# Front of a cross-attention and FFN kernel: value banks, turns of the ring, and new orders on all engines

## The reference

```python
x = x + xattn(layernorm(x), ctx, ctx, Wq, bq, Wk, bk, Wv, bv, Wo, bo)
x = x + ffn(layernorm(x), gate_w, gate_z, gate_s, up_w, up_z, up_s, down_w, down_z, down_s)

# xattn, per sample:  q = Wq @ x + bq (64 x 512), k and v from ctx alike
# heads split the 512 columns into 8 times 64
scores = einsum('hbdk,hbek->hbde', qh, kh) / sqrt(64)
out    = Wo @ (softmax(scores) @ vh) + bo
# ffn:  W = (int_w - zeros) * scales, per group of 128 rows; 512 -> 1792 -> 512
ffn(x) = (silu(x @ gate) * (x @ up)) @ down
```

## Time and profile before

| | us |
|---|---|
| time, median of 3 runs | 416.19 (416.04 to 419.14) |
| the profiled execution | 416.88 |
| its span in the trace | 415.1 |
| TensorE busy | 399.7 (96%) |
| VectorE busy | 333.5 (80%) |
| ScalarE busy | 323.5 (78%) |
| GpSimd busy | 263.6 (64%) |
| first gate/up matmul of the main part | 44.73 |

### The profile page before, as it was taken

How to read it: one execution, slowest core, us unless ns; L and a number is a source line. 1 busy time by engine, 2 the same in 40 slices (tenths; PEclk the granted TensorE clock), 3 DMA queues, 4 the chain that set the end, 5 groups by cost and what they waited for, 6 DMA issues and landing times.

```text
span 415.1 us, 10255 instructions
## 1 busy us (share of the span) xinstructions
PE 399.7 (96%) x3923; PEld 315.1 (76%) x3923; DVE 333.5 (80%) x587; ACT 323.5 (78%) x534; POOL 263.6 (64%) x283
## 2 busy tenths in 40 slices
PE   8988999999899999999999999999999999999994
PEld 5866778787677778777778778787778788888872
DVE  3677558889799978899899778898996768877676
ACT  2545898787678888787689888787799999999970
POOL 5374598677977665576667665665766666566550
PEclk9999999999999999999999999999999999999999
DMA  6399999985980010342222000242111002320003
GB/s 222 115 276 199 285 271 267 277 269 115 251 231 27 2 25 4 98 158 87 86 86 77 2 25 2 89 142 77 60 46 51 0 2 76 128 76 26 2 1 101
DMA packets 40250, 44.97 MB, mean 108 GB/s; under 512 B 3810, under 2 KB 29578, under 8 KB 40202
## 3 DMA queue, kind: packets, MB, share of 16 engines
q1 hardware_dynamic: 32242, 36.87, 27.2%
q0 software_dynamic: 7456, 7.34, 11.2%
q10 hardware_dynamic: 504, 0.11, 0.1%
HBM read 35.34 MB, written 8.97 MB: 107 GB/s over the span
## 4 chain that ended last, share of the span: by engine, by line
PE 75%; DVE 8%; issue 5%; POOL 5%; DMA 4%; SPq 0%; POOLq 0%; ACT 0%; DVEq 0%
PE banks L906 22%; PE banks L908 20%; PE banks L919 10%; PE banks L920 10%; PE banks L793 3%; DVE yT L1194 3%; DMA yT<-in_L_ffn_down_z 2%; DMA wgu<-in_L_ffn_up_w 2%; PE banks L810 2%; PE banks L850 2%; PE banks L938 2%; PE banks L839 1%; PE banks L820 1%; POOL hr L510 1%; PE banks L828 1%
## 5 line engine op out<-in xcount | busy, mean ns | idle before, releaser
L678 ACT ACTIVATE banks<-banks,ratio 128x512 f32<-128x512 f32 x336 | 207.2, 661 | 37.2 <-PE banks L908 27.5
L906 PE MATMUL banks<-xT,wgu 128*128 128x512 f32 x448 | 180.2, 402 | 1.5 <-issue 0.9
L1194 DVE SCALAR_TENSOR_TENSOR yT<-banks,sd,yT 128x512 f32<-128x512 f32 x208 | 153.1, 744 | 35.2 <-PE banks L920 34.8
L908 PE MATMUL banks<-xT,wgu 128*128 128x512 f32 x448 | 174.8, 390 | 0.0
L497 POOL TENSOR_TENSOR t_sb<-t_sb,u_sb 128x512 f32<-128x512 f32 x56 | 73.7, 1316 | 64.9 <-DVE t_sb L1179 64.6
L906 PEld LDWEIGHTS banks<-xT,wgu 128*128 128x128 f32 x448 | 84.0, 188 | 23.8 <-issue 3.0
L908 PEld LDWEIGHTS banks<-xT,wgu 128*128 128x128 f32 x448 | 84.2, 188 | 15.7
L919 PE MATMUL banks<-hr,wd 128*128 128x512 f32 x224 | 87.9, 392 | 1.6 <-POOL hr L510 1.6
L920 PE MATMUL banks<-hr,wd 128*128 128x512 f32 x224 | 87.3, 390 | 0.0
L510 POOL TENSOR_TENSOR hr<-t_sb,hr 128x512 fp32r<-128x512 f32 x56 | 73.6, 1315 | 5.1 <-ACT hr L700 0.7
L919 PEld LDWEIGHTS banks<-hr,wd 128*128 128x128 f32 x224 | 42.0, 188 | 12.0 <-DVE yT L1194 2.2
(11 more groups left out here) (114 smaller groups left out, 386.8 us busy)
## 6 DMA issues: line engine op xcount, KB each, us to landing
wgu<-z_out SPq DMA_DIRECT2D x14, 512.0 KB, 6.2
swap_d<-xn SPq DMA_DIRECT2D x18, 256.0 KB, 2.0
x_sb<-swap_d SPq DMA_DIRECT2D x72, 64.0 KB, 2.0
x_sb<-in_x SPq DMA_DIRECT2D x16, 256.0 KB, 5.1
out<-x_sb SPq DMA_DIRECT2D x16, 256.0 KB, 2.2
wgu<-in_L_ffn_gate_w POOLq DMA_DIRECT2D x7, 512.0 KB, 10.9
wgu<-in_L_ffn_up_w POOLq DMA_DIRECT2D x7, 512.0 KB, 11.7
wd_in<-in_L_ffn_down_w SPq DMA_DIRECT2D x7, 512.0 KB, 9.0
```

What stands on the lines that cost most here:

```text
L678: act.activation(banks[:, bank, :], banks[:, bank, :], ACT.Copy, scale=ratio[:, m, g, it:it + 1]).then_inc(done[n % 2], 1)
L906: pe.matmul(banks[:, bank, :], w, xT[:, c % 2, 0, g, :], start=g == 0, stop=False, skip_group_check=True)
L908: pe.matmul(banks[:, bank, :], w, xT[:, c % 2, 1, g, :], start=False, stop=True, skip_group_check=True).then_inc(full[n % 2], 1)
L1194: dve.scalar_tensor_tensor(y, bank, sd[:, it, b:b + 1], y, ALU.mult, ALU.add).then_inc(s_free, 1)
```

## The change

The banks of the values: `values(t)` of the front wrote banks 6 and 7 and now writes banks 4 and 5, for tile 3 banks 2 and 3. The third turn of the ring (tile 2) goes to bank 5 instead of bank 4, and the first turns wait accordingly. On all four computing engines the calls of the front stand in a new order, and TensorE stirs at fewer places. SyncE's order is the same.

```diff
@@ banks and ring
             if kind == "QK":
                 return 0 if t < PRE else 2 if t == PRE else 6
+            if kind == "V":
+                return 6 if t >= PRE else 4 if t < PRE - 1 else 2
             return 2 if t < PRE and kind == "S" else 6
...
             if slot[u] < PRE:
-                return RING_BANK
+                return RING_BANK + (slot[u] == PRE - 2)
...
             if s < PRE:
-                return s
+                return (0, 1, 0)[s]
@@ GpSimd
+            prepare()
             weigh(0)
-            prepare()
             weigh(1)
             add_weights(0)
+            add_weights(1)
+            rstd(0, 4)
             rstd(1, 0)
             weigh(2)
-            add_weights(1)
+            add_weights(3)
             add_weights(2)
+            weigh(3)
             rstd(1, 1)
-            weigh(3)
             rstd(1, 2)
             ratios()
-            rstd(0, 4)
             rstd(1, 3)
-            add_weights(3)
@@ ScalarE
             norm1(0)
             take_qk(0)
-            norm1(1)
             act.wait_ge(s_zraw, 32)
             act.activation(z_neg, z_raw.bitcast(I32), ACT.Copy, scale=-1.0).then_inc(s_zneg, 1)
-            norm1(2)
-            power_of(0)
+            norm1(1)
             act.wait_ge(s_trs, 1)
...
-                if h == 0:
-                    take_qk(PRE)
-
+            take_qk(PRE)
             act.wait_ge(s_prep, 1)
@@ TensorE
-                    mm = pe.matmul(banks[o, 6 + b, 256:512], wT[r, 0, :], ctx_of(t)[r, g * 256:(g + 1) * 256],
+                    mm = pe.matmul(banks[o, pair("V", t) + b, 256:512], wT[r, 0, :], ctx_of(t)[r, g * 256:(g + 1) * 256],
...
-            stir(2)
-            score(0)
-            project_wide(1)
-            stir(2)
             pe.wait_ge(s_sc, 48)
...
-            stir(1)
+            score(0)
+            project_wide(1)
             pe.wait_ge(s_wT, 3)
+            pe.wait_ge(s_scl, 2)
             values(0)
...
@@ VectorE
...
-            rest_x(0)
-            shift(1, 1)
+            shift(0, 4)
             residual(2)
             stats(1, 2)
-            stats(0, 4)
+            shift(1, 1)
+            rest_x(0)
             shift(1, 2)
-            rest_x(1)
-            shift(0, 4)
             residual(3)
             stats(1, 3)
+            rest_x(1)
+            shift(1, 3)
             rest_x(2)
-            shift(1, 3)
             take_qk(4, 0)
```

More of the change, by code:

```diff
@@ L637, in take_v @@
                     act.wait_ge(s_bA, t - 1)
-                act.activation(v_sb[:, t % 2, :, :], banks[:, 6:8, 256:512], ACT.Identity,
+                at = pair("V", t)
+                act.activation(v_sb[:, t % 2, :, :], banks[:, at:at + 2, 256:512], ACT.Identity,
                                bias=bvo[:, 0:1]).then_inc(s_v, 1)
@@ L719, in _ @@
             act.copy(sd[:, :, :].rearrange("p g c -> p (g c)"), banks[:, 4, ng:ng + NI * NC]).then_inc(s_scl, 1)
+            norm1(2)
+            power_of(0)
             take_qk(1)
-            norm1(3)
             act.wait_ge(s_wT, 3)
             take_v(0)
+            norm1(3)
             power_of(1)
+            take_qk(2)
             take_a(0)
-            take_qk(2)
-            take_qk(3)
             take_v(1)
             power_of(2)
+            take_qk(3)
             take_a(1)
             norm2(0)
+            take_v(2)
             power_of(3)
-            take_v(2)
+            take_a(2)
+            take_v(3)
+            norm1(4)
             take_x(0)
-            take_a(2)
+            take_a(3)
             norm2(1)
-            take_v(3)
+            norm2(2)
             take_x(1)
-            take_a(3)
-            norm2(2)
-            norm1(4)
             take_x(2)
@@ L978, in _ @@
             score(1)
-            stir(1)
-            stir(1)
-            wait_qk(pe, 1)
             project_wide(2)
-            pe.wait_ge(s_v, 1)
+            pe.wait_ge(s_sub, 2)
+            stir(1, 2)
             mix(0)
+            score(2)
             apply(0)
-            pe.wait_ge(s_sub, 2)
-            wait_qk(pe, 2)
-            score(2)
+            values(1)
             project_wide(3)
-            stir(1)
             pe.wait_ge(s_x1, 1)
-            values(1)
-            stir(1)
-            stir(1)
-            stir(2)
-            pe.wait_ge(s_v, 2)
             mix(1)
             pe.wait_ge(s_sub, 3)
+            stir(2, 2)
             score(3)
             apply(1)
+            values(2)
+            stir(2, 0)
             pe.wait_ge(s_x1, 2)
-            values(2)
-            pe.wait_ge(s_scl, 2)
-            turn_x(0)
-            pe.wait_ge(s_v, 3)
-            mix(2)
-            stir(1)
-            apply(2)
-            stir(2)
+            mix(2)
+            pe.wait_ge(s_sub, PRE)
+            values(3)
+            stir(2, 0)
+            apply(2)
+            turn_x(0)
+            stir(2, 0)
             pe.wait_ge(s_x1, 3)
-            values(3)
-            stir(3)
+            mix(3)
+            stir(3, 0)
+            apply(3)
             turn_x(1)
-            pe.wait_ge(s_v, 4)
-            mix(3)
-            stir(1)
-            apply(3)
-            stir(2)
-            stir(3)
-            stir(1)
             turn_x(2)
-            stir(1)
-            pe.wait_ge(s_sub, PRE)
             project_wide(PRE)
-            pe.wait_ge(s_free, PRE - 1)
             for h, (n, done) in enumerate(((s_lastn, s_lastX), (s_xn2, s_full))):
+                pe.wait_ge(s_free, (PRE - 2, PRE - 1)[h])
                 pe.wait_ge(n, (1, PRE)[h])
@@ L1031, in _ @@
                 mm.then_inc(done, 1)
-            stir(3, U_BANK[0])
+            stir(2, U_BANK[0])
             for q in range(PLACES):
@@ L1222, in _ @@
             shift(0, 0)
+            stats(0, 1)
             dve.wait_ge(s_brow, 1)
             dve.tensor_copy(bqk[:, :, :].rearrange("p m o -> p (m o)"), banks[:, 7, 0:2 * D]).then_inc(s_bqk, 1)
-            stats(0, 1)
             stats(0, 2)
+            shift(0, 1)
             dve.wait_ge(s_bqk, 1)
             take_qk(0, 0)
-            shift(0, 1)
             stats(0, 3)
             shift(0, 2)
+            take_w(1)
+            dve.tensor_copy(bvo[:, :], banks[:, 7, 4 * D:4 * D + 2]).then_inc(s_wT, 1)
             most(0)
             less_max(0)
+            shift(0, 3)
             take_qk(1, 0)
-            take_w(1)
-            dve.tensor_copy(bvo[:, :], banks[:, 7, 4 * D:4 * D + 2]).then_inc(s_wT, 1)
-            shift(0, 3)
             invert(0)
@@ L1241, in _ @@
             take_qk(2, 0)
+            invert(1)
+            most(2)
             dve.wait_ge(s_wT, 3)
             residual(0)
-            most(2)
-            invert(1)
-            take_qk(3, 0)
             less_max(2)
             stats(1, 0)
+            take_qk(3, 0)
+            stats(0, 4)
             invert(2)
```

## The result

The changed kernel takes 413.82 us (median of 9 runs, 411.9 to 415.59), the kernel before beside it 417.63 (9 runs, 415.77 to 419.14). The ratio is 0.9901, 95% interval 0.9876 to 0.9926: some 4.1 us less by the ratio, 3.8 by the medians. The forecast was 417.4, no change that a measurement can tell; what happened is a gain of 1%, between rival B (415.4) and rival C (410.0 to 412.0). The profiled execution took 413.61 (span 411.8) against 416.88 (span 415.1).

A forecast was written before the change was run, and what follows sets the result against it. Two chains, the front's ladder and a DMA chain, were taken to meet at tile 5's projection burst; 416.88 - 0.8 (DMA chain) + 2.0 (clock fall) = 418.1 profiled, 417.4 median. The 8-in-10 range was 411.0 to 420.2.

The forecast's parts named there:

- rival B: DMA chain holds the burst as in the main forecast, but the clock stays full: 415.4 us, chance 0.25.
- rival C: Down zeros land at 43.3 to 45.3 and most of the front's gain goes through: 410.0 to 412.0 us, chance 0.20.
- Two chains: The front's ladder and a chain of DMAs meet before tile 5's projection burst at 52.43 us.
- the burst of tile 5: TensorE's projection burst in the early main part, at 52.43 before; forecast at 51.6, a gain of 0.8 us.
- the ladder: Front's projection, scores, mix, apply per attention tile; first gate/up matmul forecast at 38.95, 5.8 us earlier than 44.73.
- the DMA chain: Adds 0 and 1, then zeros and down loads; down zeros forecast at 48.7 instead of 49.53, gaining 0.8 us.
- 5.4 us of hole: TensorE's idle time before tile 5's burst, waiting for the down zeros: forecast 5.4 us instead of 0.45.
- a hole under 2 us: Sign before tile 5's burst that the forecast is wrong: the DMA count was wrong and rival C holds.
- Two blocks of zeros and two of adds at 235 per us: DMA queues from 25.6 us: 8.7 us of packets plus 1.5 to landing, so `s_wgu[1]` at 35.8 instead of 38.00.
- The reason behind the sum: The two DMA queues take turns, so an add put in earlier slows the loads beside it.
- a fall after 5.4 us of idling: TensorE's clock falls to 1.2 GHz in the hole before tile 5's burst, costing 0 to 4 us, taken as 2.0.
- the signs named beforehand: Trace milestones in ladder, DMA and TensorE given as tests, such as a 4 to 6 us hole before tile 5's burst.

The follow-up runs named there:

- late_adds: Changed kernel with GpSimd issuing add 1 behind weigh(2) and add 3 behind the last rstd, as before the change; 412.89 us, ratio 0.9898.
- before_again: The kernel before, unchanged, run and profiled once more; 418.2 us.
- adds_alone: Kernel before with only the DMA side of the change: zero points negated earlier, adds 1 and 3 issued earlier; 417.29 us, ratio 0.997.
- before_subs_late: Kernel before with VectorE's first two zero-point subtractions moved behind steps 5 and 7 instead of 2 and 4; 418.25 us, ratio 1.0.
- old_negate: Changed kernel with ScalarE's negation of the zero points put behind norm1(1) again; 415.53 us, one run.
- subs_late: Changed kernel with VectorE's first two zero-point subtractions moved behind steps 5 and 7 instead of 2 and 4; 413.14 us, ratio 0.9868.
- held_zeros: Changed kernel with SyncE holding the zero loads until apply(0) is done; 422.7 us.
- shifted: Changed kernel with two stirring matmuls ahead of the first projection replaced by 34 matmuls of 16 columns; 429.3 us.

## Why the prediction was wrong, point by point

**What bounds it: right.** Two chains meet at the burst of tile 5; what it gains goes through to the end.

**The two chains: the ladder was worked out 1.75 us too early, the DMA chain 2.3 us too late.** The forecast had 5.4 us of hole; 5.4 - 1.75 - 2.3 = 1.35, and 1.34 was there. By the forecast's own sign, a hole under 2 us, the DMA count was wrong; that rival C would then hold did not come true.

**The ladder.** This execution ran 1.14 ahead of that of before from the start (transposes at 10.23 where I began at 11.37). Less that, the steps were forecast at 17.8 for mix(0), 24.2 for apply(1), 27.2 for mix(2), and 37.8 for the first gate/up matmul; they came at 17.83, 27.23, 28.92 and 40.70. mix(0) is exact; at the end 2.9 us are missing. Up to mix(2) it is 1.7, most of the first gap and 0.3 of the second; from there to gate/up it is 1.1, of which 0.7 is the third gap. The other 0.4 lies in steps without a gap (11.03 in late_adds against 10.65 by the forecast). A row of this kind did stand in the trace of before, but small: 0.42, in apply(2) (0.72 in before_again). The old ladder can have a large one too: its crossing in apply(0), two pages earlier, cost nothing in the two profiles of before, 0.18 in adds_alone and 1.28 in before_subs_late. Why it varies so is not shown.

**The DMA chain: the step that failed.** "Two blocks of zeros and two of adds at 235 per us ... `s_wgu[1]` at about 35.8": it landed at 33.83, 2.0 earlier, and that decided the size of the hole. From there to the down zeros I had 12.9 and it took 12.57. Of the 2.0 some 1.1 is this execution's earlier start (add 0 went out at 19.94, forecast 21.0), and some 0.5 is that its first packets came some 4 us later, not 4.6. The rest is the count of packets. The DMA queues of the changed kernel in 24 to 32, in which the 1024 packets of both adds went through:

```profile
q0 software_dynamic: 1025, 1.02, 81.3%
q1 hardware_dynamic: 753, 0.75, 33.3%
```

Together that is 222 per us, no faster than the 235 of the forecast. But only 753 packets of loads went in this time, not 1024: the last add did not have both blocks of zeros ahead of it, and so the flow took 8.0 us, not 8.7 (from its end to the landing it was 1.8, forecast 1.5). The start of the zero loads is not what set `s_wgu[1]`: in old_negate the zero points went out 0.62 later and it landed at 33.38. The reason behind the sum was right: late_adds shows that issuing add 1 seven us earlier lands it 0.55 earlier. And it shows what the early add 3 costs: from `s_wgu[1]` to the down zeros it takes 10.5 us there and 12.57 in the changed kernel, 2.1 more (forecast 1.4 more than before).

**The clock: a term for a fall that did not come.** 2.0 us were put down for a fall after 5.4 us of idling. No fall followed 1.34 us; one followed 2.83 (old_negate), so the mechanism is there. What the forecast did not have is that the clock falls in the front of the old order too, in three of its four profiles, and in the two of after it does not. Summing with the measured burst, 416.88 - 3.1 gives 413.8, and 413.61 was profiled. The forecast's 418.1 for a profiled execution is these 2.3 of the DMA chain and 2.0 of clock away from it; the ladder's 1.75 cost no time of their own, since the DMA chain still held the burst.

**The baseline.** One profile of before was read as the kernel. It had a late start (score(0) at 12.00, 10.82 in before_again), which made it slower, and no fall of the clock, which made it faster; the other three profiles with the old ladder have the fall. At the burst the two nearly cancel: 52.43 and 53.44. So luck has a part in these numbers. Of the 3.14 us at the burst some 1.1 are the start; the change itself gained some 2.0 there, where the forecast had 0.8, so that 1.2 of the 2.3 us of the DMA chain are an error of the sum. And the 2.2 us of the fall, of which the medians may hold a part, were in no row.

**The rivals.** C had the right sign, with zeros that land earlier, but needed 43.3 to 45.3; B had the full clock. The truth lies between the two at 46.40. The range of 411.0 to 420.2 held 413.82; a gain clear of noise had a chance of 0.18. Of the signs named beforehand, the first gate/up matmul (40.70, said 38 to 40), `s_wgu[1]` (33.83, said 35 to 37), the down zeros (46.40, said 47.5 to 50) and the hole (1.34, said 4 to 6) all missed; mix(3) came at 32.50, where about 32 was said.

## What to carry to other kernels

Where two chains meet and each is worked out from many steps, the idle time between them is a small difference of large sums: here errors of 2 us in each made a hole of 5.4 out of 1.34, so a cost that hangs on the length of that hole must not decide the forecast. Read a second profile of the same kernel before the first one is taken for its baseline. A rung that is packed more densely while the DMA queues are full can run into its own instruction fetch: look for idle time put down to issue at equal counts of instructions, and then whether another wait would have stood in the same place. Compare milestones from the first common instruction, not from the start of the span: the two profiles of before differ by 1.2 us in where that lies.

## What the runs showed of the hardware

- TensorE stood 0.17 to 2.01 us at many crossings of 256 instructions in the ladder while zero loads and adds filled the queues, and not at all at others (the second in subs_late and old_negate). At the first two crossings it did not stand where the loads were held back (held_zeros).
- The start has two speeds in the same program: the eight matmuls of the first projection take 1.05 us or 1.91 (1.74 in before), and score(0) comes at 10.6 to 10.8 or at 12.0 to 12.7. The granted clock reads 1.00 there in both, so the view of the clock does not show it; the durations do.
- Ahead of a slow start, matmuls of 16 columns took 0.214 us each (14.53 / 68); the eight matmuls of the projection behind them took 1.91 us, at 20.92.
- Holes of 1.34 and 1.75 (after) and of 2.01 us (subs_late) left the granted clock at 1.00; 1.80 (shifted) and 2.83 (old_negate) were followed by a fall, and so were waits of 0.71 and 1.28 close together (before_subs_late). The length of one hole does not decide it.
